# Adding the two sign tiles of each weight chunk in an accumulating DMA instead of on VectorE

## The reference

```python
def _weight_quant(w):
    scale = 1.0 / jnp.clip(jnp.mean(jnp.abs(w)), 1e-05)
    wq = jnp.clip(jnp.round(w * scale), -1.0, 1.0) / scale
    return w + jax.lax.stop_gradient(wq - w)
...
x = _layernorm(x + _L0_attn_ref(x, L0_attn_w_qkv, L0_attn_w_out), axis=-1)
gate = jax.nn.silu(_bitlinear(x, w_gate))          # _bitlinear also rounds x to 8 bits
up = _bitlinear(x, w_up)
x = _layernorm(x + _bitlinear(gate * up, w_down), axis=-1)
```

## Time and profile before

| What | Value |
|---|---|
| median of 2 runs | 2862.01 us (2854.78 to 2869.25) |
| the profiled execution, its time | 2868.73 us |
| its span on the slowest core, core 5 | 2867.1 us |
| spans of the 8 cores | 2841.8 to 2867.1 us |
| granted TensorE clock, mean over the span, by core | 0.763 to 0.769 |
| phase 4's weight chunks, on core 5 | from 1049.6 us (first sign) to 1695.7 us (last store landed) |

### The profile page before, as it was taken

One profiled execution on the slowest core, in us unless ns is written; L12 is line 12 of the kernel. 1 busy time (PEld: TensorE's weight loads), 2 busy tenths in 40 slices (PEclk: granted clock), 3 DMA queues, 4 the chain that ended last, 5 costly groups with the idle time before them and its releaser, 6 DMA issues.

```text
span 2867.1 us, 23098 instructions; the slowest of 8 cores (2841.8 to 2867.1 us)
## 1 busy us (share of the span) xinstructions
PE 1606.3 (56%) x6348; PEld 648.6 (23%) x6348; DVE 1241.5 (43%) x1983; ACT 745.1 (26%) x1177; POOL 332.3 (12%) x588
## 2 busy tenths in 40 slices
PE   0993049999999631111111109549764975597563
PEld 0441013323232210000000004224222422242221
DVE  0015543333333524334433424684457447645733
ACT  0320036666665013433433322102001100220010
POOL 1001211111111011111111110000120011001121
PEclk9997558888888555555555559869896999799787
DMA  9001223333332044554454454405421432242133
GB/s 171 13 1 30 59 74 92 95 98 107 95 99 92 18 108 143 152 143 140 139 161 150 152 176 128 131 12 160 122 81 57 160 119 77 82 147 70 55 118 102
DMA packets 152464, 295.95 MB, mean 103 GB/s; under 512 B 28291, under 2 KB 98182, under 8 KB 152070
## 3 DMA queue, kind: packets, MB, share of 16 engines
q0 software_dynamic: 57344, 191.14, 23.6%
q1 hardware_dynamic: 94998, 103.34, 11.5%
HBM read 250.13 MB, written 46.14 MB: 103 GB/s over the span
## 4 chain that ended last, share of the span: by engine, by line
PE 44%; DMA 17%; DVE 17%; issue 7%; ACT 7%; DVEq 4%; another core or an unknown queue 3%; POOL 2%; ACTq 0%; SPq 0%; POOLq 0%
DMA h_td<-ternd 7%; PE p6a L1524 7%; PE p6a L1538 7%; PE p_sc L425 6%; PE p_av L442 6%; PE p6a L1498 6%; PE p_qk L206 4%; PE p_sc L432 3%; DMA t_wst<-wuT 3%; DMA t_wst<-wgT 2%; ACT a_E L453 2%; DMA t_wst<-wdT 2%; PE p_qk L220 2%; PE p_R L685 2%
## 5 line engine op out<-in xcount | busy, mean ns | idle before, releaser
L453 ACT ACTIVATE a_E<-p_sc 128x512 bf16<-128x512 f32 x640 | 333.9, 632 | 195.4 <-PE p_sc L432 108.4
L1498 PE MATMUL p6a<-h_td,h_hqT 128*128 128x512 bf16 x1024 | 273.7, 419 | 152.1 <-DMA h_td<-ternd 140.4
L425 PE MATMUL p_sc<-a_q,a_k 64*128 64x512 bf16 x640 | 242.1, 418 | 180.4 <-DMA e_sel<-sel 151.3
L1524 PE MATMUL p6a<-h_tg,h_xql 128*128 128x512 bf16 x1024 | 249.1, 387 | 91.1 <-DMA h_tu<-ternu 48.7
L858 PE MATMUL p_o<-f_wout,d_aor 128*128 128x512 bf16 x256 | 87.6, 519 | 339.5 <-DVE f_y L919 339.5
L1538 PE MATMUL p6a<-h_tu,h_xql 128*128 128x512 bf16 x1024 | 243.7, 381 | 0.0
L911 DVE TENSOR_TENSOR t_tn<-t_ta,t_tb 128x1024 bf16<-128x1024 bf16 x96 | 64.9, 689 | 325.5 <-ACT t_tb L998 325.5
L1322 ACT ACTIVATE h_sg<-p6a,h_sc 128x512 bf16<-128x512 f32 x128 | 88.3, 690 | 426.1 <-PE p6a L1524 320.1
L1452 POOL DMA_DIRECT2D h_td<-ternd x128 | 92.3, 721 | 920.1 <-PE p6a L1498 903.6
L466 DVE TENSOR_REDUCE t_msum<-t_wst 128x1 f32<-128x1024 f32 x96 | 116.0, 1219 | 188.3 <-DMA t_wst<-wdT 66.2
L994 ACT ACTIVATE t_ta<-t_wst,p_thr 128x1024 bf16<-128x1024 f32 x96 | 109.8, 1143 | 318.6 <-DMA t_wst<-wuT 120.1
(11 more groups left out here) (129 smaller groups left out, 1853.9 us busy)
## 6 DMA issues: line engine op xcount, KB each, us to landing
t_wst<-wgT POOLq DMA_DIRECT2D x64, 512.0 KB, 5.7
t_wst<-wuT POOLq DMA_DIRECT2D x64, 512.0 KB, 5.7
t_wst<-wdT POOLq DMA_DIRECT2D x64, 512.0 KB, 4.8
h_td<-ternd POOLq DMA_DIRECT2D x128, 256.0 KB, 3.2
h_tg<-terng SPq DMA_DIRECT2D x32, 1024.0 KB, 6.2
h_tu<-ternu SPq DMA_DIRECT2D x32, 1024.0 KB, 8.9
f_xt<-x SPq DMA_DIRECT2D x16, 512.0 KB, 5.0
y1s<-f_y1n SPq DMA_DIRECT2D x16, 512.0 KB, 2.6
```

The costliest lines, as they stand in the source:

```text
L425: mm = t.matmul(pb[:], s_k[hp * 64: hp * 64 + 64, ch * S + kc * 128: ch * S + (kc + 1) * 128], s_q[hp * 64: hp * 64 + 64, ch * S + j * 512 ...
L453: se.inc(s.activation(s_E[:, kc * 512:(kc + 1) * 512], p_sc[kc % 4][:], AF.Exp, bias=-CSTAB, scale=0.125))
L1498: mm = t.matmul(p_a[k][:], s_hqT[k][:, kc * 128:(kc + 1) * 128], s_td[dn % 2][:, kk * 512:(kk + 1) * 512], start=(g2 == 0 and kk == 0), st ...
L1524: mm = t.matmul(pg[:], s_xql[j % 2][:, kc * 512 + k * 128:kc * 512 + (k + 1) * 128], s_tg[gs % 2][:, kc * 512:(kc + 1) * 512], start=(kc = ...
```

## The change

The add of t_ta and t_tb leaves VectorE. GpSimd now issues, for each chunk, a DMA inside the core's memory that reads t_tb and adds it into t_ta. It waits for that DMA to land and then stores t_ta to DRAM. The tiles t_tn are gone. ScalarE's signs of chunk i now wait for the store of chunk i-2 to land, where they waited for its add. Two new semaphores, dAcc0 and dAcc1, count the adding DMAs; tv2 stays at zero and is no longer waited for. The loads, their buffers and the order between load and store in GpSimd's list are as before.

```diff
             for i6 in range(NWCH):
...
                 dW5[L % 3].dinc(g.dma_start(out=s_wst[L % 3][:],
                                             in_=WCHUNKS[i6][1]))
                 if i6 >= 1:
-                    g.wait_ge(tv2.h, i6)
-                    dTst[(i6 - 1) % 4].dinc(g.dma_start(
-                        out=WCHUNKS[i6 - 1][2], in_=s_tn[(i6 - 1) % 4][:]))
-            g.wait_ge(tv2.h, NWCH)
-            dTst[(NWCH - 1) % 4].dinc(g.dma_start(
-                out=WCHUNKS[NWCH - 1][2], in_=s_tn[(NWCH - 1) % 4][:]))
+                    p6 = i6 - 1
+                    g.wait_ge(ts2.h, 2 * p6 + 2)
+                    dAcc[p6 % 2].dinc(g.dma_start(
+                        out=s_ta[p6 % 2][:], in_=s_tb[p6 % 2][:],
+                        accum_op=ALU.add))
+                    g.wait_ge(dAcc[p6 % 2].h, ((p6 // 2) + 1) * 16)
+                    dTst[p6 % 4].dinc(g.dma_start(
+                        out=WCHUNKS[p6][2], in_=s_ta[p6 % 2][:]))
+            p6 = NWCH - 1
...                                   # the same add, wait and store for the last chunk
@@ VectorE
-            def _combs(v, hi):
-                while tern_emitC[0] < hi:
-                    i6 = tern_emitC[0]
-                    v.wait_ge(ts2.h, 2 * i6 + 2)
-                    if i6 >= 4:
-                        v.wait_ge(dTst[i6 % 4].h, ((i6 - 4) // 4 + 1) * 16)
-                    tv2.inc(v.tensor_tensor(s_tn[i6 % 4][:], s_ta[i6 % 2][:],
-                                            s_tb[i6 % 2][:], ALU.add))
-                    tern_emitC[0] += 1
...
-                _combs(v, ((nt + 1) * NWCH) // NT)
-            _combs(v, NWCH)
@@ ScalarE, _signs
                     if i6 >= 2:
-                        s.wait_ge(tv2.h, i6 - 1)
+                        s.wait_ge(dTst[(i6 - 2) % 4].h,
+                                  (((i6 - 2) // 4) + 1) * 16)
```

More of the change, by code:

```diff
@@ L135, in build_program @@
         dTst = [Ctr(f"dTst{i}") for i in range(4)]
+        dAcc = [Ctr("dAcc0"), Ctr("dAcc1")]
         dXql = [Ctr("dXql0"), Ctr("dXql1")]
@@ L297, in _ @@
                 dS.dinc(sy.dma_start(out=dbg["vsb"], in_=s_v[:]))
-        ctrs = ([dS, dC2, dG, dO, dAor, dWo, dTst[0], dTst[1], dTst[2], dTst[3], dXql[0], dXql[1], dOut, te, ve, se, ge, tpA, thrV, thrT, ts2, tv2]
+        ctrs = ([dS, dC2, dG, dO, dAor, dWo, dTst[0], dTst[1], dTst[2], dTst[3], dAcc[0], dAcc[1], dXql[0], dXql[1], dOut, te, ve, se, ge, tpA, thrV, thrT, ts2, tv2]
                 + dDen + dRst + dX + dY1n + dXq + dW5 + dGu + dTd + dY1l)
@@ L333, in build_program @@
                 for i in range(2)]
-        s_tn = [mk(scD, f"t_tn{i}", [128, 1024], BF16, side="right")
-                for i in range(4)]
         WCHUNKS = []
@@ L779, in _ @@
                 if i6 >= 1:
-                    g.wait_ge(tv2.h, i6)
-                    dTst[(i6 - 1) % 4].dinc(g.dma_start(
-                        out=WCHUNKS[i6 - 1][2], in_=s_tn[(i6 - 1) % 4][:]))
-            g.wait_ge(tv2.h, NWCH)
-            dTst[(NWCH - 1) % 4].dinc(g.dma_start(
-                out=WCHUNKS[NWCH - 1][2], in_=s_tn[(NWCH - 1) % 4][:]))
+                    p6 = i6 - 1
[7 more added lines that the diff above has]
+            p6 = NWCH - 1
+            g.wait_ge(ts2.h, 2 * p6 + 2)
+            dAcc[p6 % 2].dinc(g.dma_start(
+                out=s_ta[p6 % 2][:], in_=s_tb[p6 % 2][:], accum_op=ALU.add))
+            g.wait_ge(dAcc[p6 % 2].h, ((p6 // 2) + 1) * 16)
+            dTst[p6 % 4].dinc(g.dma_start(
+                out=WCHUNKS[p6][2], in_=s_ta[p6 % 2][:]))
         dG_wout = dWo.n
@@ L876, in build_program @@
         assert te_tr_end == trun4 == te4_0 + 4 * NT
-        tern_emitC = [0]
         @block.vector
@@ L1046, in build_program @@
                        (ts2.h, ts2.n), (tv2.h, tv2.n),
+                       (dAcc[0].h, dAcc[0].n), (dAcc[1].h, dAcc[1].n),
                        (dW5[0].h, dW5[0].n), (dW5[1].h, dW5[1].n),
```

## The result

The changed kernel takes 3012.5 us (median of 11 runs, 2994 to 3038) and the kernel before 2865.6 (median of 10). The ratio is 1.052, with a 95% interval of 1.048 to 1.056: 147 us slower. The forecast was 2891 us and a change within 2%. The time lies inside the range, 2820 to 3020, near its upper end. Of the two cases that the prediction held equally likely, 0.42 each, the forecast was the wrong one: the second rival came true, the slow adding DMA with GpSimd's list as the bound.

What follows compares the result with a forecast made beforehand. The prediction took latency round a loop in the weight chunks as the bound. Row tiles of 632.0 us, last chunks 35 and ending 8.2 made 675 against 646, 29 us more: forecast 2891 us, range 2820 to 3020.

Steps and rivals of the forecast that it cites:

- the second rival: Weight chunks: adding DMA slow, GpSimd's list the bound, from A = 5.5 on; 3123 us at A = 7.5; chance 0.42.
- VectorE's lateness: Weight chunks: VectorE, busy in the quantising chain, reaches its adds late, costing about 9 us per row tile.
- The sum with L and A: Row tile of six weight chunks: 3A + 2L + 17.9, giving 43.0 us in wgT and wuT, 40.0 in wdT.
- L: Time from issue to landing of a 512 KB weight load: 5.2 us for wgT and wuT, 4.9 for wdT.
- A: Time from issue to landing of an adding DMA: 4.9 us for wgT and wuT, 4.1 for wdT.
- the rival's loop: GpSimd's strict order of adding DMA, wait, store, load: at least A + 1.9 us per chunk.
- the forecast's formula: Row tile of six chunks as two pairs of L + A + 4.1 and one of A + 9.7: 3A + 2L + 17.9.
- the pair of chunks: Loop of load, signs, adding DMA, store and next load, coming back every two chunks: L + A + 4.1 us.
- the bursts: DMA bursts from VectorE's late adds, expected to go; in wgT and wuT taken to cancel against the second operand, A staying 4.9.
- threshold of 5.5 (4.7 for wdT): Value of A in us from which the kernel would be slower by more than 2%; 0.6 above the 4.9 assumed.
- ScalarE's new wait: Signs of chunk i wait for the store of chunk i-2; costed at nothing, store landing in 2.7 us, load in 4.8.
- The decoupling: Weight chunks: adding DMA lands like an unhindered store, A = 2.7, a gain of 64 us to 2798 us; chance 0.12.

Runs made afterwards that it cites:

- x2_noadd: Changed kernel without any add, t_ta stored as it is (weights wrong): 2692 us, ratio 0.943 to the kernel before.
- x7_before_deep: Kernel before, add still on VectorE, load of chunk p+3 sent once chunk p is signed, ahead of the wait for its add: 2701 us, ratio 0.945.
- x1_copy: Changed kernel with a plain copy of t_tb onto t_ta in place of the adding DMA (weights wrong): 2941 us, ratio 1.028 to the kernel before.
- x3_gap: Changed kernel with GpSimd also waiting, ahead of every adding DMA, for the load just sent to land: 3174 us, one execution.
- x4_gapcopy: As x3_gap, with a plain copy of t_tb onto t_ta in place of the adding DMA (weights wrong): 3122 us, one execution.
- x5_addfirst: Changed kernel with the adding DMA of chunk p sent ahead of the load of chunk p+2: 2791.6 us, ratio 0.975 to the kernel before.
- x6_addfirst3: As x5_addfirst, with three loads ahead instead of two: 2793.1 us, ratio 0.975 to the kernel before.

## Why the prediction was wrong

**What bounds the kernel, and VectorE's lateness: right.** The reading of the loop, that VectorE costs it time by being late and not by its 0.69 us, is borne out by x2_noadd (166 us for taking the adds out) and, from the other side, by x7_before_deep (167 us for sending the loads ahead with VectorE left as it is). Neither number is the lateness alone; the late pair of the tile in x7_before_deep gives it by itself, 8.3 us against the prediction's 9.

**The sum with L and A: right in form.** With the measured A = 6.2, the rival's loop, 96 x (6.2 + 1.9) + 5 = 783 us, meets the 792 of core 3. In part that is luck: the loop adds means and I put in a median. By GpSimd's timeline the mean of A is about 6.5, 0.3 more, and the other terms are 1.7 and not 1.9. For x1_copy, where A is 4.8, the forecast's formula gives 3 x 4.8 + 2 x 5.2 + 17.9 = 42.7 per row tile, 7.1 per chunk, against 7.3, so 20 to 25 us of that kernel's chunks are in terms that the sum has too small. The prediction puts the hand-over from one loop to the other at A = L + 0.3. The runs agree on both sides of it: with 6.2 against an L of 5.5 GpSimd doesn't wait for signs, with 4.8 against 5.2 it does 78 times. No run lies near the point itself.

**The size of A: wrong, and this is the step that failed.** I put A at 4.9 in wgT and wuT and 4.1 in wdT; it was 6.2 and 6.4 in the first two and 6.1 in the last (core 3, by stretch). The term was too small by 1.3 to 2.0 us, and with that the pair of chunks was the wrong loop to add up. The failure has two parts. The first is that I took medians of stores from a loop in which the stores have other neighbours. Before, a store is sent ahead of its load. The adding DMA is sent behind one. I said so in the rival, and wrote against it that "when it falls behind by less, two more us of distance bring 7.5 to 4.7". That misreads the rows: the two stores went out 0.5 and 1.3 us behind their loads, 0.8 us apart. And in the loop the distance isn't even 1.3: the timeline above has it at 0.5 to 0.8 each time, since a late adding DMA finds the next signs ready and the next one follows the load at once. A row for that place was there, 7.5 at 0.5 us, and I used it only as a bound; taken as A it would have given the rival's 3123 us, 110 too much, so it had the right loop and not the right size. The second part is the price of adding: I let it cancel against the bursts. It is 1.0 us undisturbed; in the list the difference is 1.4, with the copy some 0.7 us farther behind its load (x3_gap, x4_gapcopy, x1_copy).

The consequence is steeper than the error: 1.3 to 2.0 us on A per chunk turned 29 us into 148, as the prediction's own threshold of 5.5 (4.7 for wdT) foretold. The time is inside the range because its upper end was worked out with an A of 6.8 (5.6 for wdT).

**L: nearly right.** 5.5 and 5.8 for wgT and wuT, 5.3 for wdT, against 5.2 and 4.9; in the loop that came to hold it doesn't count.

**ScalarE's new wait: right for this kernel.** The signs wait for loads [waits above], and the stores land earlier, 3.2. In x5_addfirst the cover is gone and it shows.

**The other rivals.** The decoupling would have won with A = 2.7. That is near what the Trainium skill ("DMA: Bandwidth & Descriptors", Anatomy of one DMA) gives for 256 KB, 2.6 us. The undisturbed copy landed in 2.3 and so agrees with it within 0.3; the same copy behind a store and a load landed in 4.8, and it is this place that counts. "Collectives: The Full Stack", Part 3, in the Trainium skill, has a reducing transfer at half of a copy's rate. Here queue 0's packets took, in the mean of the eight cores, 667 us of the 16 engines' time in the kernel before, 859 in the changed one and 768 in x1_copy: of 96 DMAs that is 2.0 us for an adding one and 1.1 for a copy, a ratio of 1.9. Undisturbed they took 836 us (x3_gap) and 773 (x4_gapcopy), 1.8 and 1.1 each, a ratio of 1.6. The traces bear it out in the direction, and in size with 1.6 and 1.9 (the 0.9 and 2.2 us of the expectations are from the slowest cores). The estimate that the prediction drew from it, 5.8 us, came nearer to the measured 6.2 than my own 4.9.

**What stays open.** Of the 2.9 us of place, the load of 512 KB ahead has the most: the last adding DMA of the changed kernel has only the store 1.1 us ahead of it and lands like an undisturbed one, 3.3 (one DMA per core, eight cores), and in x5_addfirst, with a store 0.5 us or more ahead and the load behind, it is 3.9. No run has only the load ahead, and none shows whether the adding DMA waits in the queue or shares the engines with the load. And x5_addfirst does not separate the shorter adding DMA from the earlier load.

## What to carry to other kernels

Before work moves from an engine into a DMA, look at what stands ahead of that DMA in its queue: a transfer that something waits for belongs in front of the prefetch, and the duration to put in the sum is that of rows with the same neighbours, not the median of its size. One such row isn't enough: here the single store 0.5 us behind a load took 7.5 us and the adding DMA 6.2. When an engine that is late holds up a loop, ask first what has not been sent because of it; sending that earlier (x7_before_deep, 5.5%) can be worth as much as taking the work off the engine (x2_noadd, 5.7%), and here it took no more than another order of one engine's list. In a serial list of one engine, issue, wait, issue, the loop has no slack to spread out, so assume the closest spacing that the list permits.

## What the runs showed of the hardware

- A 256 KB bf16 DMA inside the core's memory that adds lands in 3.3 us undisturbed, a copy in 2.3. Its issue keeps GpSimd for about 0.9 us (x3_gap: 883 ns median), that of the copy for 0.54 (x4_gapcopy: 536 ns).
- The adding DMA, 0.5 us behind a 512 KB load and 1.1 behind a 256 KB store in GpSimd's queue, lands in 6.2 us; the copy, 1.2 behind the load and 1.7 behind the store, in 4.8 (x1_copy). With the store alone ahead, 1.1 us, the adding DMA lands in 3.3.
- GpSimd needs about 0.5 us from a landed DMA to its next issue, ScalarE 0.1 from a landed load to its next operation. From the chain that ended last in the kernel after, core 4 (start, us, what), between the adding DMA's landing and the store's issue:

```profile
1306.16 5.93 DMA t_ta<-t_tb
1312.09 0.02 issue
1312.11 0.02 POOLq L784
1312.13 1.42 issue
1313.55 0.02 POOLq L775
```

- Here it is 1.4 us instead of the usual 0.48, and stretches of this kind come up now and then in all the kernels. The Trainium skill ("SBUF — State Buffer", SBUF: two separate sides, the trap "DVE blocks DMA") has VectorE's two-port operations keep GpSimd from writing descriptors. That can't be the reason here, for VectorE ran nothing at the time. Its next operation on that core:

```profile
1314.24 0.27 DVE L924 TENSOR_SCALAR f_st<-f_st,c_consts 128x1 f32<-128x1 f32 x1 [35.35 <-ACT f_tr L1001]
```

- In x5_addfirst one such stretch ends within 0.02 us of the end of a VectorE operation, and so does one in x6_addfirst3:

```profile
1385.05 0.81 DVE L951 TENSOR_SCALAR f_z<-f_y1n,f_st,c_consts 128x1024 f32<-128x1024 f32 x1
1385.88 0.89 POOL L782 DMA_DIRECT2D t_ta<-t_tb  x1 [3.28 <-issue]
```

- The signs for this DMA were ready at 1384.36, so it is 1.0 us later than GpSimd's usual 0.5. That would fit the trap, but no experiment took the VectorE operation away. It isn't the cause of the result either: of the 17 waits of this kind ahead of x5_addfirst's adding DMAs, 10.9 us in all, twelve are only the usual 0.55 us behind the signs.
